# A spiking layer with a mixture of eight experts: two chains of term sums joined by a DMA, and the bias product read straight from PSUM one beat later

## The chip, the core and the metric

The kernel runs on one core of one Trainium2 chip. The metric is the device time of one execution in microseconds (us), lower is better. Engines are named as in the profile: PE is TensorE, PEld its weight loads, DVE is VectorE, ACT is ScalarE, POOL is GpSimd, SP is SyncE.

## The reference, cut to what matters

The input x has 16 sequences of 512 time steps with 256 channels. Per layer the reference computes:

```
R, K, V = x @ Wr.T, x @ Wk.T, x @ Wv.T
for t:  v += (in - v) * 0.5;  s = (v >= 1);  v *= 1 - s      # LIF, for r, k, v
        h = 0.9 * h + k * v;  y = r * h
x1  = layernorm(x + y @ Wo.T) * g1 + b1
s1  = lif_scan(x1 @ W1.T + b1)                               # 256 -> 1024
ffn = lif_scan(s1 @ W2.T + b2)                               # 1024 -> 256
x3  = layernorm(x + layernorm(x1 + ffn) * g2 + b2)
gates = softmax(x3 @ Wg + bg);  the two largest, normalised
out = sum over the two chosen experts e of gate_e * (x3 @ We[e] + be[e])
result = layernorm(x3 + out)
```

Everything is float32. The kernel multiplies all eight experts for every token and scales each by its gate, which is zero for six of them. The change lies in the last two lines: how the eight terms and the gated bias are added up to `res`, the input of the last layernorm.

## The kernel before, in words

**Chunks and beats.** Time is cut into 32 chunks of 16 steps; a chunk is 256 tokens (16 steps by 16 sequences), two tiles of 128. The whole kernel is a software pipeline of beats, k = -2 to 38. A chunk passes its stages in successive beats, and each stage has a lag: load of x (-2), R/K/V products (-1), LIF (0), attention output and LayerNorm 1 (1), W2 (3), LayerNorm 2 and 3 (LAG_Z, 5), experts (LAG_M, 6), final sum and last LayerNorm (LAG_F, 7). So in one beat TensorE works on the experts of chunk k-6 and VectorE on the final sum of chunk k-7. Beats 7 to 32 have all stages ("steady"); beats 33 to 38 lose one after the other ("drain"). Every engine has one hand-written order of work per beat (its `beat` function), and semaphores count stages.

**VectorE's slots.** VectorE runs the LIF recurrence, 32 instructions per beat (16 `membrane`, L723, and 16 `reset`, L730), and after each of them a slot of side work (`side`, slots -1 to 31). The tables STEADY, FILL and DRAIN say which side work stands in which slot. Of this: `y` in slots 0 to 4, `z_sum` and `fin_sum` in slot 5 (in the drain both in slot -1, with the spikes of h1, `s`, L1092, between them), `ln1_sum` (L831) in 7, `ln2_scale` in 16 and 17, the LN3 shift and `fin_add` in 24 (14 and 15 in the drain).

**The experts' terms.** Float32 products are made from split halves (hi and lo, float32r): three matmuls for each 128x128 block. Expert 0's product is scaled and added to x3 by VectorE into `acc` (`add_e0`, L937). ScalarE scales expert 1's product into `odd_sum` and the others' into `term` (`read_expert`, L596). GpSimd then adds them by DMA: terms 2, 4, 6 to `acc` (`add_even`, L1179) and terms 3, 5, 7 to `odd_sum` (`add_odd`, L1190), each an accumulating DMA of 256 KB from SBUF to SBUF that waits for the landing of the one before it in its chain. Terms 2 and 3 are added in the experts' beat, 4 to 7 in the beat after. The last chunk's terms are added by VectorE (`add_expert`, L950) in beat 37.

**The bias.** TensorE multiplies the transposed gates by the stacked expert biases (`biases`, L471) into `ps_zx`, behind expert 7, the last work of its beat. `ps_zx` is one PSUM bank with three users in turn: the transposes of z for LayerNorm 2 (`z_T`, tile `ps_zx<-cst,z`, L393), the transposes of x3 (`ps_zx<-cst,x`), and the bias.

**The final sum** (`fin_stage`). Step 0, `fin_sum` (L969): VectorE adds `ps_zx` to term 7 in SBUF; it waits for the bias and for all terms. TensorE's `z_T` of that beat waits for it, and so does the odd add of term 7. Step 1, `fin_add` (L976): `res = acc + odd_sum`, after both chains have landed. Steps 2 to 4: statistics, their aggregate (L810), the shift (L822); in between GpSimd computes the reciprocal deviation (L1147, L1149). ScalarE normalises `res` and sends it out. In the last beat, 38, the final sum is `res = acc + ps_zx` (L963).

**GpSimd's order in a steady beat**: spikes of h1 (L1161), add_even 4, add_odd 5, the DMA of the residual x into xb (L1195), reciprocal of LN1, add_even 6, reciprocal of LN2, add_odd 7, reciprocal of LN3, add_even 2, reciprocal of the final one, add_odd 3, the low half of the next x (L1168). In the drain the spikes are VectorE's.

## Time and profile before

| | us |
|---|---|
| median of 3 runs | 1047.85 |
| lowest, highest | 1046.26, 1048.25 |
| profiled execution, its own time | 1046.27 |
| span of its instructions | 1044.5 |
| mean granted TensorE clock | 0.969 of full speed |

A row of the timeline gives the start of a group of instructions in us from the span's start, its length, engine, line, operation and output<-input, and in brackets the idle time of the engine before it with what ended it. A row of the groups of lines has the count, the busy time in us, the mean of one in ns, and the idle time before them. Accumulating DMAs are issued by GpSimd (0.9 us of its time each) and land some time later; the landing is when their semaphore has its full count. Ends of matmuls are modelled, so rows of TensorE that follow each other overlap a little.

### The profile page before, as it was taken

Reading aid. Unit: us, or ns where it says so; the run is one execution under the profiler, and the core shown is the slowest. Engines: PE = TensorE matmul, PEld = TensorE weight load, DVE = VectorE, ACT = ScalarE, POOL = GpSimd, SP = SyncE. Lnnn points to the kernel's source line nnn. Section 1 sums busy time; section 2 is a strip of 40 time slices with the busy share of each in tenths; the row PEclk is TensorE's granted clock in tenths of the full one; section 3 lists DMA queues with packets and bytes.
Section 4 is the critical chain, followed back from the end, with each engine's and each line's share of the span. In section 5 each row is a group of like instructions: output and inputs, shape, how many; then the busy total and the mean of one; then the engine's idle time right before and its main releaser. Section 6 shows DMA issues by size and latency. Waiting matters only on the chain.

```text
span 1044.5 us, 22651 instructions
## 1 busy us (share of the span) xinstructions
PE 954.2 (91%) x7552; PEld 926.6 (89%) x7552; DVE 955.0 (91%) x3860; ACT 543.0 (52%) x1256; POOL 576.8 (55%) x720
## 2 busy tenths in 40 slices
PE   4577779999999999999999999999999999899884
PEld 4567769999999999999999999999999999889784
DVE  6888898999999999999999999999999999988875
ACT  4333333455666555555666555555566555456461
POOL 1001122676666666677666666667666666764551
PEclk8878888999999999999999999999999999999998
DMA  4310112454445445444445545444445554446762
GB/s 159 97 51 31 31 41 52 73 110 92 92 91 112 102 102 109 97 101 98 89 88 112 102 105 108 99 95 99 92 87 109 102 109 95 91 92 117 138 128 65
DMA packets 53110, 98.30 MB, mean 94 GB/s; under 512 B 5889, under 2 KB 5889, under 8 KB 52993
## 3 DMA queue, kind: packets, MB, share of 16 engines
q0 software_dynamic: 31392, 57.16, 31.6%
q1 hardware_dynamic: 16992, 31.30, 9.7%
q10 hardware_dynamic: 4608, 8.39, 2.1%
q8 instruction: 60, 0.98, 0.4%
q14 instruction: 58, 0.47, 0.1%
HBM read 31.29 MB, written 8.39 MB: 38 GB/s over the span
## 4 chain that ended last, share of the span: by engine, by line
PE 68%; DVE 17%; ACT 5%; DMA 5%; issue 3%; POOL 2%; POOLq 0%; DVEq 0%; SPq 0%; ACTq 0%
PE ps_e L349 25%; PE ps_proj L349 11%; PE ps_proj L419 9%; PE ps_proj L404 7%; PE ps_attn L385 6%; PE ps_proj L425 5%; DVE U L723 4%; DVE V L730 3%; DMA acc<-term 3%; ACT odd_sum L596 2%; PE ps_zx L393 2%; DVE stats L804 2%; DVE h L774 2%; ACT x_hi L577 1%; DVE x1n L831 1%
## 5 line engine op out<-in xcount | busy, mean ns | idle before, releaser
L349 PE MATMUL ps_e<-we_hi,x_hi 128*128 128x256 f32 (+1 forms) x1024 | 295.5, 289 | 16.8 <-ACT odd_sum L596 14.9
L349 PE MATMUL ps_e<-we_lo,x_hi 128*128 128x256 f32 (+1 forms) x1024 | 286.9, 280 | 0.0
L349 PE MATMUL ps_e<-we_hi,x_lo 128*128 128x256 f32 (+1 forms) x1024 | 286.7, 280 | 0.0
L730 DVE SCALAR_TENSOR_TENSOR V<-U 128x256 f32<-128x256 f32 (+5 forms) x656 | 243.3, 381 | 0.6
L723 DVE SCALAR_TENSOR_TENSOR U<-V,U 128x256 f32<-128x256 f32 (+5 forms) x656 | 234.0, 367 | 1.8
L559 ACT ACTIVATE U<-ps_proj,cst 128x256 f32<-128x256 f32 x320 | 135.6, 481 | 167.4 <-PE ps_proj L425 83.9
L1147 POOL TENSOR_SCALAR veps<-mv 128x2 f32<-128x2 f32 x128 | 55.7, 435 | 300.4 <-DVE mv L810 300.0
L349 PEld LDWEIGHTS ps_e<-we_hi,x_hi 128*128 128x128 f32 x1024 | 192.5, 188 | 23.0 <-ACT odd_sum L596 20.9
L1161 POOL TENSOR_SCALAR s<-U 128x256 fp32r<-128x256 f32 x208 | 192.0, 948 | 13.4 <-DVE V L730 13.4
L349 PEld LDWEIGHTS ps_e<-we_hi,x_lo 128*128 128x128 f32 x1024 | 192.9, 188 | 0.1
L349 PEld LDWEIGHTS ps_e<-we_lo,x_hi 128*128 128x128 f32 x1024 | 192.3, 188 | 0.0
L596 ACT ACTIVATE term<-ps_e,gate 128x256 f32<-128x256 f32 x372 | 157.0, 478 | 49.6 <-PE ps_e L349 49.3
L547 ACT ACTIVATE U<-ps_proj 128x512 f32<-128x512 f32 x96 | 57.5, 599 | 185.3 <-PE ps_proj L349 178.7
L419 PE MATMUL ps_proj<-x_hi,w_hi 128*128 128x256 f32 x512 | 135.3, 285 | 6.4 <-ACT x_hi L577 6.4
L419 PE MATMUL ps_proj<-x_hi,w_lo 128*128 128x256 f32 x512 | 134.2, 283 | 0.0
L404 PE MATMUL ps_proj<-s,w_hi 128*128 128x256 f32 x512 | 122.2, 280 | 2.9 <-POOL s L1161 2.9
L349 PE MATMUL ps_proj<-x_hi,wrkv_hi 128*128 128x256 f32 x384 | 114.2, 298 | 9.0 <-DVE wrkv_lo L1130 6.2
L404 PE MATMUL ps_proj<-s,w_lo 128*128 128x256 f32 x512 | 121.8, 279 | 0.0
L425 PE MATMUL ps_proj<-x_lo,w_hi 128*128 128x256 f32 x512 | 106.8, 290 | 4.0 <-DVE x_lo L852 3.9
L774 DVE SCALAR_TENSOR_TENSOR h<-h,kv 128x32 f32<-128x32 f32 x512 | 109.1, 213 | 1.4 <-DVE kv L767 0.5
L349 PE MATMUL ps_proj<-x_hi,wrkv_lo 128*128 128x256 f32 x384 | 110.0, 286 | 0.0
L349 PE MATMUL ps_proj<-x_lo,wrkv_hi 128*128 128x256 f32 x384 | 109.9, 286 | 0.0
(87 smaller groups left out, 2182.3 us busy)
## 6 DMA issues: line engine op xcount, KB each, us to landing
acc<-term POOLq DMA_DIRECT2D x93, 256.0 KB, 3.6
odd_sum<-term POOLq DMA_DIRECT2D x93, 256.0 KB, 3.3
xt<-x_T SPq DMA_DIRECT2D x33, 256.0 KB, 3.0
xa<-x_tok SPq DMA_DIRECT2D x32, 256.0 KB, 4.3
xb<-cst SPq DMA_DIRECT2D x32, 256.0 KB, 2.3
xb<-x_tok POOLq DMA_DIRECT2D x32, 256.0 KB, 6.2
out<-res ACTq DMA_DIRECT2D x32, 256.0 KB, 2.1
term<-w SPq DMA_DIRECT2D x8, 256.0 KB, 5.5
```

The source lines that it names most:

```text
L349: mm = pe.matmul(dst, lhs, rhs, start=(i == 0), stop=(i == n - 1))
L385: mm = pe.matmul(ps_attn[:, j, :], y[:, k * N + j * P:k * N + (j + 1) * P], wo[:, k, :], start=(k == 0), stop=(k == DK - 1))
L404: mm = pe.matmul(ps_proj[:, bank, e, :], wp[:, c:c + P], s1[:, ft, :], start=(ft == 0 and part == 0), stop=(ft == FK - 1 and part == 1))
L419: pe.matmul(ps_proj[:, bank, e, :], wp[:, cols(k, e)], x1_hi[:, k, :], start=(k == 0 and wp is w1_hi), stop=False)
L425: mm = pe.matmul(ps_proj[:, bank, e, :], w1_hi[:, cols(k, e)], x1_lo[:, k, :], start=False, stop=(k == DK - 1))
L547: return nc.scalar.activation(out_, in_, ACT.Identity)
L559: last = nc.scalar.activation(dst[:, :, col + e * B:col + (e + 1) * B], ps_proj[:, bank, e, :].rearrange("p (t b) -> p t b", b=B), ACT.Ide ...
L596: last = nc.scalar.activation(dst[:, j * D:(j + 1) * D], ps_e[:, bank, j, :], ACT.Identity, scale=gate[:, b.slot(LAG_M, 2), j, e:e + 1])
L723: v.scalar_tensor_tensor(out=U[:, s, t, c0:c1], in0=V[:, c0:c1], scalar=0.5, in1=U[:, s, t, c0:c1], op0=ALU.mult, op1=ALU.add).then_inc(do ...
L730: v.scalar_tensor_tensor(out=V[:, c0:c1], in0=u, scalar=THRESHOLD, in1=u, op0=ALU.is_lt, op1=ALU.mult).then_inc(done, 1)
L774: op = v.scalar_tensor_tensor(out=h[:, t, :], in0=h[:, (t - 1) % STEPS, :], scalar=DECAY, in1=kv[:, t, :], op0=ALU.mult, op1=ALU.add)
L1161: last = g.tensor_scalar(s1[:, ft, :].rearrange("p (t b) -> p t b", b=B), U[:, (b.k - 1) % 2, :, COL_H1 + ft * B:COL_H1 + (ft + 1) * B], T ...
```

## The change

- `fin_sum` is gone from VectorE and from the three slot tables; FIN_STEPS goes from 7 to 6.
- GpSimd has a new step `join`, right behind the odd add of term 7 and ahead of the reciprocal of LN3: it waits for the last landing of both chains and then adds `odd_sum` to `acc` by one more accumulating DMA of 256 KB. The odd add of term 7 no longer waits for `fin_sum`.
- The final sum is now `res = acc + ps_zx` in all beats; it waits for the bias and for the join's landing (in beat 38 for the terms).
- The bias product moves on TensorE from the end of the experts' beat to the next beat, between expert 3 and W1, and waits there until `ln2_scale` has read both tiles of `ps_zx`. The last chunk's stays in beat 37, ahead of expert 7, and waits for the final sum of the chunk before.
- `z_T` no longer waits for the sum of the chunk in LAG_F; the transposes of x3 now do, since the bias stands in `ps_zx` until the final sum has read it.

```diff
-STEADY = dict(y=(0, 1, 2, 3, 4), z_sum=5, spikes_h1=7, fin_sum=5,
+STEADY = dict(y=(0, 1, 2, 3, 4), z_sum=5, spikes_h1=7,
...
-FILL = dict(z_sum=-1, y=(-1,) * 5, spikes_h1=-1, fin_sum=-1,
+FILL = dict(z_sum=-1, y=(-1,) * 5, spikes_h1=-1,
...
-DRAIN = dict(z_sum=-1, y=(-1,) * 5, spikes_h1=-1, fin_sum=-1,
+DRAIN = dict(z_sum=-1, y=(-1,) * 5, spikes_h1=-1,
...
@@ -267,9 +267,10 @@
         gateT_done, gateT_ready, bias_done = sem("gateT_done"), sem("gateT_ready"), sem("bias_done")
         e0_added, term_ready = sem("e0_added"), sem("term_ready")
         even_added, odd_added = sem("even_added"), sem("odd_added")
+        joined = sem("joined")
         fin_steps, x3_ready, res_ready = sem("fin_steps"), sem("x3_ready"), sem("res_ready")
 
-        Y_STEPS, LN1_STEPS, LN2_STEPS, LN3_STEPS, GATE_STEPS, FIN_STEPS = 2, 7, 8, 5, 15, 7
+        Y_STEPS, LN1_STEPS, LN2_STEPS, LN3_STEPS, GATE_STEPS, FIN_STEPS = 2, 7, 8, 5, 15, 6
         ADDED = 16 * (E // 2 - 1)
         GATES_DONE = 13
 
@@ -459,13 +460,15 @@
                     mm = pe.transpose(ps_attn[0:STACK, j, 0:P], gate_parts[:, j, :].bitcast(F32), ident)
                 mm.then_inc(gateT_done, 1)
 
-            def biases(b):
-
-                pe.wait_ge(gateT_ready, b.value(1, LAG_M, 1))
+            def biases(b, lag):
+
+                pe.wait_ge(gateT_ready, b.value(1, lag, 1))
 
                 if b.has(LAG_Z):
-                    pe.wait_ge(x3_lo_ready, b.value(1, LAG_Z, 1))
-                if b.k == LAG_M:
+                    pe.wait_ge(ln2_steps, b.value(LN2_STEPS, LAG_Z, 6))
+                if lag == LAG_M:
+                    pe.wait_ge(fin_steps, b.value(FIN_STEPS, LAG_F, 1))
+                if b.k == LAG_F:
                     pe.wait_ge(bias_lo_ready, 1)
                 for j in range(TILES):
                     mm = pe.matmul(ps_zx[:, j, :], gate_T[:, j, :], bias_stack[:], start=True, stop=True)
@@ -474,8 +477,6 @@
             def z_T(b):
 
                 pe.wait_ge(z_ready, b.value(2, LAG_Z, 2))
-                if b.has(LAG_F):
-                    pe.wait_ge(fin_steps, b.value(FIN_STEPS, LAG_F, 1))
                 transpose4(ps_zx, lambda j, k: z[:, k, j * P:(j + 1) * P], zT_done)
 
             def beat(b):
@@ -519,6 +520,8 @@
                 if b.has(LAG_M):
                     for e in (2, 3):
                         expert(b, e)
+                if b.has(LAG_F) and b.k < LAST_BEAT:
+                    biases(b, LAG_F)
                 if b.has(LAG_Y):
                     if b.k == LAG_Y:
                         pe.wait_ge(split_lo, W1_PIECES)
@@ -528,15 +531,15 @@
                 if b.has(LAG_Z):
 
                     pe.wait_ge(x3_ready, b.value(1, LAG_Z, 1))
+                    if b.has(LAG_F):
+                        pe.wait_ge(fin_steps, b.value(FIN_STEPS, LAG_F, 1))
                     transpose4(ps_zx, lambda k, j: x3[:, j, k * P:(k + 1) * P], x3T_done)
                 if b.has(LAG_M):
                     gates_T(b)
                     for e in (5, 6, 7):
                         if e == 7 and b.last_m:
-                            biases(b)
+                            biases(b, LAG_M)
                         expert(b, e)
-                    if not b.last_m:
-                        biases(b)
 
             run_beats(beat)
 
@@ -954,33 +957,22 @@
 
             def fin_stage(b, step):
                 chain = lambda n: after(fin_steps, FIN_STEPS, LAG_F, b, n)
-                if step == 0 and b.k == LAST_BEAT:
-                    return
-                if step == 1 and b.k == LAST_BEAT:
+                if step == 1:
                     dve.wait_ge(bias_done, b.value(1, LAG_F, 1))
-                    dve.wait_ge(term_ready, b.value(E - 1, LAG_F, E - 1))
-                    dve.wait_ge(out_stored, b.value(16, LAG_F))
-                    v.tensor_tensor(res[:], acc[:, b.slot(LAG_F, 2)], ps_zx[:], ALU.add).then_inc(fin_steps, 2)
-                    return
-                if step == 0:
-                    dve.wait_ge(bias_done, b.value(1, LAG_F, 1))
-                    dve.wait_ge(term_ready, b.value(E - 1, LAG_F, E - 1))
-                    last_term = term[:, E - 3, 0:PIECE].rearrange("p (j d) -> p j d", j=TILES)
-                    v.tensor_tensor(last_term, last_term, ps_zx[:], ALU.add).then_inc(fin_steps, 1)
-                if step == 1:
-                    dve.wait_ge(even_added, b.value(ADDED, LAG_F, ADDED))
-                    dve.wait_ge(odd_added, b.value(ADDED, LAG_F, ADDED))
+                    if b.k == LAST_BEAT:
+                        dve.wait_ge(term_ready, b.value(E - 1, LAG_F, E - 1))
+                    else:
+                        dve.wait_ge(joined, b.value(16, LAG_F, 16))
 
                     if some(b.value(16, LAG_F)):
                         dve.wait_ge(out_stored, b.value(16, LAG_F))
-                    v.tensor_tensor(res[:], acc[:, b.slot(LAG_F, 2)], odd_sum[:, b.slot(LAG_F, 2)],
-                                    ALU.add).then_inc(fin_steps, 1)
+                    v.tensor_tensor(res[:], acc[:, b.slot(LAG_F, 2)], ps_zx[:], ALU.add).then_inc(fin_steps, 1)
                 if step == 2:
-                    chain(2)
+                    chain(1)
                     for j in range(TILES):
                         bn_stats(3, j, res[:, j, :], fin_steps)
                 if step == 3:
-                    bn_aggr(b, 3, fin_steps, FIN_STEPS, LAG_F, 4)
+                    bn_aggr(b, 3, fin_steps, FIN_STEPS, LAG_F, 3)
                 if step == 4:
                     mean_shift(b, 3, fin_steps, LAG_F)
 
@@ -1008,8 +1000,6 @@
                             y_stage(b, step)
                 if b.has(LAG_S) and b.dve_spikes and slot == at["spikes_h1"]:
                     spikes_h1(b)
-                if b.has(LAG_F) and slot == at["fin_sum"]:
-                    fin_stage(b, 0)
                 if b.has(LAG_Z):
                     for j in range(TILES):
                         if slot == at["ln2_stats"][j]:
@@ -1185,10 +1175,16 @@
 
                 if some(b.value(ADDED, lag, 16 * (e // 2 - 1))):
                     pool.wait_ge(odd_added, b.value(ADDED, lag, 16 * (e // 2 - 1)))
-                if e == E - 1:
-                    pool.wait_ge(fin_steps, b.value(FIN_STEPS, lag, 1))
                 g.dma_start(odd_sum[:, b.slot(lag, 2)].rearrange("p j d -> p (j d)"), term[:, e - 2, 0:PIECE],
                             accum_op=ALU.add).then_inc(odd_added, 16)
+
+            def join(b):
+
+                pool.wait_ge(even_added, b.value(ADDED, LAG_F, ADDED))
+                pool.wait_ge(odd_added, b.value(ADDED, LAG_F, ADDED))
+                g.dma_start(acc[:, b.slot(LAG_F, 2)].rearrange("p j d -> p (j d)"),
+                            odd_sum[:, b.slot(LAG_F, 2)].rearrange("p j d -> p (j d)"),
+                            accum_op=ALU.add).then_inc(joined, 16)
 
             def add_bias(b):
                 pool.wait_ge(xb_loaded, b.value(16, LAG_Z, 16))
@@ -1215,12 +1211,13 @@
                     reciprocal_std(b, 1, ln2_steps, LN2_STEPS, LAG_Z, 4)
                 if sums:
                     add_odd(b, LAG_F, 7)
+                    join(b)
                 if has_z:
                     reciprocal_std(b, 2, ln3_steps, LN3_STEPS, LAG_Z, 4)
                 if has_m and not b.last_m:
                     add_even(b, LAG_M, 2)
                 if has_f:
-                    reciprocal_std(b, 3, fin_steps, FIN_STEPS, LAG_F, 6)
+                    reciprocal_std(b, 3, fin_steps, FIN_STEPS, LAG_F, 5)
                 if has_m and not b.last_m:
                     add_odd(b, LAG_M, 3)
                 if b.has(LAG_X):
```

## Rows read from the trace of the kernel before

**Rows 1.** Page, part 1: busy us, share of the span and instructions of TensorE and VectorE.

```profile
PE 954.2 (91%) x7552; PEld 926.6 (89%) x7552; DVE 955.0 (91%) x3860; ACT 543.0 (52%) x1256; POOL 576.8 (55%) x720
```

**Rows 2.** Windows, 328 to 884 us; columns as the first line names them.

```profile
core 0: us, PE busy (x) PEld busy (x) DVE busy (x) ACT busy (x) POOL busy (x), PEclk, DMA share, GB/s
328.00:884.00 556.00, 547.87 (x4478) 537.72 (x4477) 533.78 (x2068) 315.59 (x740) 369.55 (x456) 1.00 0.48 100
```

**Rows 3.** Waits, 328 to 884 us: us in total, times, longest us.

```profile
DVE x1n L831 <- PE ps_attn L385: 9.8, 17, 0.6
...
PE ps_e L349 <- ACT odd_sum L596: 8.1, 19, 0.4
```

**Rows 4.** Timeline, VectorE's final sums of beats 33 to 37: start us, us.

```profile
959.55 0.68 DVE L976 TENSOR_TENSOR res<-acc,odd_sum 128x512 f32<-128x512 f32 x1
...
978.16 0.69 DVE L976 TENSOR_TENSOR res<-acc,odd_sum 128x512 f32<-128x512 f32 x1
...
995.63 0.69 DVE L976 TENSOR_TENSOR res<-acc,odd_sum 128x512 f32<-128x512 f32 x1
...
1011.66 0.69 DVE L976 TENSOR_TENSOR res<-acc,odd_sum 128x512 f32<-128x512 f32 x1
...
1026.94 0.68 DVE L976 TENSOR_TENSOR res<-acc,odd_sum 128x512 f32<-128x512 f32 x1
```

**Rows 5.** Timeline, TensorE, its wait in beat 34 (idle us before, releaser).

```profile
970.24 0.63 PE L393 MATMUL ps_zx<-cst,z 128*128 128x128 f32 x4 [2.90 <-DVE term L969]
```

**Rows 6.** Groups of lines, VectorE: xcount | busy us, mean ns.

```profile
L969 DVE TENSOR_TENSOR term<-term,ps_zx 128x512 f32<-128x512 f32 x31 | 20.9, 676 | 8.2 <-ACT term L596 8.2
...
L963 DVE TENSOR_TENSOR res<-acc,ps_zx 128x512 f32<-128x512 f32 x1 | 0.7, 689 | 1.7 <-DMA out<-res 1.7
```

**Rows 7.** Timeline, VectorE, one steady beat: final sum, then y.

```profile
503.89 0.69 DVE L976 TENSOR_TENSOR res<-acc,odd_sum 128x512 f32<-128x512 f32 x1
...
513.35 0.94 DVE L797 SCALAR_TENSOR_TENSOR y<-U,h 128x256 f32<-128x256 f32 x2
```

**Rows 8.** Timeline, TensorE, the same beat: transposes of x3, then projection.

```profile
506.49 0.60 PE L393 MATMUL ps_zx<-cst,x 128*128 128x128 f32 x4
...
515.90 1.89 PE L385 MATMUL ps_attn<-wo,y 128*128 128x256 f32 x8
```

**Rows 9.** Timeline, GpSimd: issues of term 7's odd add.

```profile
495.74 0.93 POOL L1190 DMA_DIRECT2D odd_sum<-term  x1
...
953.23 0.92 POOL L1190 DMA_DIRECT2D odd_sum<-term  x1
...
973.50 0.93 POOL L1190 DMA_DIRECT2D odd_sum<-term  x1
```

**Rows 10.** Line L1190, issue to landing: 200 to 900 us, then beats 33 to 37.

```profile
DMA to landing us min/median/max: 3.2/3.3/6.4
...
DMA to landing us min/median/max: 5.5/5.5/5.5
...
DMA to landing us min/median/max: 3.5/3.5/3.5
...
DMA to landing us min/median/max: 3.9/3.9/3.9
...
DMA to landing us min/median/max: 4.2/4.2/4.2
...
DMA to landing us min/median/max: 3.2/3.2/3.2
```

**Rows 11.** Chain of waits, beat 35 into 36: start us, us, what.

```profile
998.49 3.30 DMA odd_sum<-term
...
1001.83 0.49 issue
```

**Rows 12.** Timeline, VectorE, beat 34: spikes of h1, then the LN2 statistics.

```profile
967.59 1.91 DVE L1092 TENSOR_SCALAR s<-U 128x256 fp32r<-128x256 f32 x8
...
970.91 0.43 DVE L804 BATCH_NORM_STATS2 stats<-ps_zx 128x6 f32<-128x256 f32 x1 [0.63 <-PE ps_zx L393]
```

## The prediction, made before the changed kernel ran

> **What bounds the kernel now.** I read the page's busy shares first. TensorE and VectorE are both busy 91% of the span [rows 1], so the shares alone do not say which one sets the time. The table of windows, asked for the even middle of the run (328 to 884 us, 19 beats), says more: TensorE is busy 547.87 of 556 us at full granted clock, VectorE 533.78 [rows 2]. The list of waits for the same window names TensorE's pauses: 8.1 us over 19 times, all for ScalarE's read of expert 1 (L596), which is 0.43 us in each beat. VectorE, in turn, waits 9.8 us for TensorE's output projection [rows 3]. So in a steady beat (some 29.3 us, 556 / 19) TensorE works back to back, VectorE follows it and has about a microsecond to spare. ScalarE's read of expert 1 comes behind TensorE's transposes of x1n; VectorE's fin_sum (L969) is nowhere in that chain.
>
> The last beats are different. The starts of the final sum (L976) in beats 33 to 37 are 18.6, 17.5, 16.0 and 15.3 us apart [rows 4]: with stages dropping out, no engine is full, and the beat is a chain through VectorE, GpSimd's queue and its accumulating DMAs. In beat 34 TensorE even stands 2.90 us still for fin_sum before it can transpose z [rows 5]. That is where a change of waits can be seen.
>
> **The change, part by part.**
>
> *Removed from VectorE: fin_sum, the add of the bias product into term 7.* 31 times 0.676 us, 20.9 us of busy time [rows 6]. In the steady beats this lies beside TensorE's work. VectorE reaches its next wait on TensorE (L831) 0.6 us sooner and waits 0.6 us longer; behind that wait nothing has moved. I cost it at zero there. If TensorE did not cover it, it would give up to 0.43 us a beat, no more, since TensorE has no more idle time.
>
> *The final sum reads ps_zx in place of odd_sum.* The kernel has both kinds of read already: with two SBUF tiles L976 takes 0.68 or 0.69 us [rows 4], and the one in the last beat with PSUM (L963) takes 0.689 us [rows 6]. Cost: zero.
>
> *The bias product one beat later.* The same two matmuls per chunk, now behind expert 3 and ahead of W1. They wait for ln2_scale to have read ps_zx, and VectorE has done this well before in a steady beat. TensorE's work is the same: zero. The new wait of the x3 transposes for the final sum has these in its way: they start at 506.49 in the beat whose final sum starts at 503.89 and takes 0.69 [rows 7, 8], so the sum may be 1.9 us late before TensorE feels it. The other limit is y: it is written by 514.29 (513.35 + 0.94) and TensorE wants it at 515.90 [rows 7, 8], 1.6 us of slack.
>
> *The join: one more accumulating DMA of 256 KB per chunk on GpSimd's queue.* It waits for the last odd add to land, costs the queue an issue (0.93 us, as the add's own [rows 9]), and the final sum waits for its landing. Three prices. (a) The flight of an odd add, issue to landing: 3.2 / 3.3 / 6.4 us (least, median, most) in the middle of the run [rows 10]. Nothing else of GpSimd's is in flight with the join, so I take 3.3 from the median; the ends are 3.2 and 6.4. (b) From a landing to the issue behind it: in the chain of waits, 3.30 us of flight from 998.49, then 0.49 us of "issue" from 1001.83, then the next add [rows 11]; I take 0.5. (c) 0.1 from the landing to VectorE.
>
> *A steady beat.* The odd add of term 7 is issued at 495.74 [rows 9]. It lands at 499.0, the join is issued at 499.5 and lands at 502.8, 1.1 us before the final sum at 503.89. Hidden. GpSimd is free again by 500.5; the reciprocals it holds up (ln3's, then the final one) are asked for later than that. A join late by up to 1.6 us is absorbed as well. So beats 7 to 32: zero.
>
> The Trainium skill (DMA: Bandwidth & Descriptors, Anatomy of one DMA) fits a GpSimd-issued DMA by 2.0 us plus bytes over 436e3 per us. For 256 KB that is an estimate of 2.6 us, while the trace shows 3.3. With 2.6 the join would be 0.7 us cheaper in each of the last beats.
>
> *The last beats.* The odd add of term 7 lands here just before the final sum, and the join has no room. Neither has the work behind it: GpSimd's ln3 reciprocal now waits behind the join too, but is back earlier than the join has landed.
> - Beat 33: issued 953.23 [rows 9], flight 5.5 [rows 10], 0.5, join 3.3, 0.1: the final sum starts at 962.6, against 959.55 [rows 4]. Late by 3.1 us. VectorE is dense from there to the spikes of beat 34, which end at 972.6 in place of 969.50 (967.59 + 1.91) [rows 12]. Here the change gives something back: fin_sum (0.6) is gone and TensorE transposes z while the spikes run, so the LN2 statistics start behind the spikes and the logits, at 972.9 in place of 970.91 [rows 12]: 2.0 late.
> - Beat 34: issued at 973.50 + 2.0, flight 3.5 [rows 9, 10], then 0.5 + 3.3 + 0.1: the final sum at 982.9 against 978.16, 4.7 late.
> - Beats 35 to 37: now a loop through the queue decides. Final sum to the odd add of term 3 takes 2.9 us (995.63 to 998.49, through GpSimd's reciprocal), then term 5 after 3.3 + 0.5, then term 7 after 3.3 + 0.5, its flight f, 0.5, the join 3.3, 0.1: together 14.4 + f, in place of intervals of 17.5, 16.0 and 15.3 [rows 4, 11]. With f = 3.9, 4.2 and 3.2 [rows 10] the final sums fall at 982.9 + 18.3 = 1001.2, + 18.6 = 1019.8 and + 17.6 = 1037.4. Against 995.63, 1011.66 and 1026.94 that is 5.6, 8.1 and 10.5 late. In beat 37 VectorE's own add of experts 4 to 7 stands behind the final sum in its queue, and so do TensorE's experts 6 and 7 and the last output: the delay goes to the end in full.
>
> **Sum:** 0 in beats -2 to 32, +10.5 us in beats 33 to 37. The profiled execution took 1046.27 us (span 1044.5), which makes 1056.8; the median of the three runs is 1.58 above it, so 1058.4.
>
> **Rivals.**
> 1. *The join is late in the steady beats too.* Place: VectorE's slot 24 in 26 beats. If it flew 5.5 us and more, as adds do that share the engines, the final sum would start 1.1 us late and more; from 1.6 us on, y is late and each beat pays. At the 6.4 of [rows 10] that is 499.5 + 6.4 + 0.1 - 503.89 = 2.1, so 0.5 us a beat, 13 us, and the last beats pay 3.1 more for each of five joins, 15.5: 1087. A middle course (5.5, nothing steady, 5 x 2.2 in the end) gives 1069. For it: the DMA engines carry one more transfer. Against: adds with a free queue fly 3.3.
> 2. *Faster: the drain gains.* If the last beats' waits overlap more than I think and the join falls under other waiting, the gain is TensorE's wait for fin_sum in beat 34, 2.90 us [rows 5]: 1045. It decides if the last odd add lands over 3.9 us before VectorE comes to the final sum. The rows speak against this: in beat 34 it lands at 977.0, 1.2 us before.
> 3. *VectorE, not TensorE, sets the steady beat.* Then fin_sum's 0.6 us comes back up to TensorE's idle 0.43: 26 x 0.43 = 11, less the loss in the end: about no change, 1047. Against: TensorE's pause waits for ScalarE alone [rows 3].
> 4. *Only one join is paid.* If the queue's loop does not close and the lag stays at beat 34's 4.7: 1052.5.
>
> **How the numbers follow.** The forecast has 0.62, the long flights (1) 0.12, the small loss (4) 0.12, no change (3) 0.07, the gain (2) 0.07. This kernel's measurement can tell about 0.2% (2.1 us) from nothing. Slower by more: 0.62 + 0.12 + 0.12 = 0.86. The forecast's own range is 1055 to 1063: flights of 4.2 in place of 3.3 add 4.5 in five joins, and a give-back of 2.90 in one more beat takes 3 off. To hold 8 in 10 I reach down to rival 4 and up to the middle course of rival 1: 1051 to 1068.
>
> **What would show it.** Right: in the steady beats the final sum starts without idle time before it and the beat stays 29.3; TensorE's waits there are ScalarE's 0.43 alone. From beat 33 on the final sum shows idle time that ends with the DMA acc<-odd_sum, some 1 to 5 us each, and the starts of the final sum in beats 34 to 37 are about 18 us apart. GpSimd shows a wait of 2.4 us for the odd add's landing before each join, and TensorE none for fin_sum. Wrong: steady beats of another length, an idle GpSimd queue behind the join that holds up ln3's shift on VectorE in steady beats, or last beats of the old length.

## The result, and the profile after

The changed kernel takes 1093.88 us (median of 4 runs, 1092.66 to 1094.57) against 1048.05 us: ratio 1.0427, 95% interval [1.0405, 1.0449]. The forecast was 1058.4, with 1068 as its upper end: slower, as forecast, but by 45.8 us in place of 10.5. The profiled execution took 1094.57 us, its span is 1092.7.

Where the 48.2 us of span came from is read from the starts of the final sums (L969 after, L976 before), which cut both spans at the same work:

| stretch | before | after | difference |
|---|---|---|---|
| start to final sum of beat 7 | 211.0 | 213.5 | +2.5 |
| to that of beat 30 (23 steady beats) | 673.6 | 710.9 | +37.2 |
| to that of beat 32 | 54.7 | 56.7 | +2.1 |
| to that of beat 37 | 87.6 | 97.2 | +9.5 |
| to the end of the span | 17.6 | 14.4 | -3.2 |

A steady beat now takes 30.91 us on the mean (710.9 / 23); it took 29.29. The windows of the changed kernel, 328 to 884 us, as in [rows 2]:

```profile
328.00:884.00 556.00, 526.17 (x4246) 513.90 (x4245) 516.63 (x1943) 298.91 (x702) 370.49 (x450) 0.99 0.51 103
```

TensorE was busy 547.87 of these 556 us and is now busy 526.17; VectorE went down too, and the granted clock is 0.99 where it was 1.00. Nobody is full, so the beat is set by a chain of waits. The waits of the same window (engine, line, what it waited for: us in total, times, longest):

```profile
POOL acc L1185 <- DMA odd_sum<-term: 54.0, 17, 4.0
...
POOL s L1151 <- DVE V L733: 29.5, 18, 2.1
...
PEld ps_e L350 <- DVE x_lo L864: 23.7, 13, 2.0
DVE res L969 <- issue: 22.2, 14, 2.5
PE ps_e L350 <- DVE x_lo L864: 21.0, 13, 1.8
...
DVE x1n L834 <- PE ps_attn L386: 5.3, 6, 1.2
...
PE ps_e L350 <- ACT odd_sum L599: 7.9, 18, 0.6
```

The last two answer to [rows 3]: ScalarE's 0.43 us a beat is still there, VectorE's wait for the projection has halved. New are TensorE's 21.0 us for the low half of x3 (behind the final sum on VectorE), VectorE's 22.2 us ahead of the final sum ("issue" means that the profile names no releaser; in 19 of the 23 steady beats the sum starts 0.08 us after the join's landing), and 29.5 us of GpSimd's spikes for VectorE's last reset. The join's flight, line L1185, from 200 to 910 us and then in one drain beat:

```profile
DMA to landing us min/median/max: 3.3/4.7/5.5
...
DMA to landing us min/median/max: 3.3/3.3/3.3
```

**The closed loop.** The chain of waits from one final sum to the next (start us, us, what) shows what none of the prediction's steps had:

```profile
400.52 0.69 DVE res L969
...
403.36 0.74 POOL rstd L1139
...
404.20 0.93 POOL odd_sum L1178
405.14 1.34 POOL x_lo L1158
406.47 2.07 issue
...
408.58 1.18 POOL s L1151 x2
...
415.99 4.45 DMA acc<-term
...
420.98 0.93 POOL acc L1169
...
422.99 3.29 DMA odd_sum<-term
...
426.81 3.34 DMA acc<-odd_sum
...
431.56 0.69 DVE res L969
```

The final sum stands in VectorE's slot 24; the resets behind it end the beat's recurrence; GpSimd's spikes wait for the last reset; adds 4, 6 and 7 stand behind the spikes on GpSimd's queue; the join behind them; the next final sum behind the join. So nothing in this chain is fixed by TensorE, and a late join moves its own next start. Its terms, against the same in the kernel before (final sums at 474.59 and 503.89):

| from | to | before | after |
|---|---|---|---|
| final sum | spikes start | 6.67 | 8.06 |
| | even add 4 issued | 7.34 | 7.41 |
| | odd add 7 issued | 7.14 | 7.00 |
| | its landing, + 0.5, join issued | (3.8) | 3.82 |
| | join lands, final sum starts | (3.4) | 4.75 |
| sum | | (28.35) | 31.04 |

In brackets the prices of the prediction. With those the loop would take 28.35 us, under the beat of 29.3. Two terms grew, 1.4 us each. By this sum either of them alone would be enough to put it over (29.7).

*The join flies 4.7 us and not 3.3.* SyncE starts two loads beside it. Its queue beside the join of the loop above:

```profile
426.80 0.47 SPq L337 DMA_DIRECT2D xb<-cst  x1
427.31 0.59 SPq L310 DMA_DIRECT2D xt<-x_T  x1
```

What they cost hangs on the order of the two. In the steady beats of the changed kernel, e2 and e5 (experiments below) 34 joins are issued 0.45 us or more ahead of SyncE's first load and fly 3.3 us at the median (3.26 to 4.45); 39 are issued later than that, and they fly 4.7 (3.63 to 5.49). In the old trace the first load starts at 500.56. The join that the prediction put at 499.5 is 1.1 us ahead of it, on the good side; a join that comes 0.7 us or more later is not.

*VectorE is held by GpSimd.* The timeline of VectorE, then of GpSimd, in the same beat:

```profile
404.35 2.41 DVE L733 SCALAR_TENSOR_TENSOR V<-U 128x256 f32<-128x256 f32 x1
406.80 0.42 DVE L726 SCALAR_TENSOR_TENSOR U<-V,U 128x256 f32<-128x256 f32 x1
...
407.47 0.68 DVE L864 TENSOR_TENSOR x_lo<-ps_zx,x_hi 128x512 fp32r<-128x512 f32 x1
```

```profile
404.84 1.64 POOL L1158 TENSOR_TENSOR x_lo<-xt,x_hi 128x512 fp32r<-128x512 f32 x1
...
408.58 7.46 POOL L1151 TENSOR_SCALAR s<-U 128x256 fp32r<-128x256 f32 x8 [2.11 <-DVE V L733]
```

A reset takes 0.42 us; this one takes 2.41 and ends with GpSimd's split of the next x (404.84 + 1.64 = 406.48, then 0.3). The kernel before has the same split, but it begins just as VectorE's own x_lo does, which reads PSUM and one SBUF tile and is not lengthened; the reset behind it stretches to 1.00. (In 4 of its 23 steady beats the split meets `kv`, L764, instead, which takes 1.3 us and not 0.23.)

```profile
508.86 0.69 DVE L861 TENSOR_TENSOR x_lo<-ps_zx,x_hi 128x512 fp32r<-128x512 f32 x1
509.46 1.00 DVE L730 SCALAR_TENSOR_TENSOR V<-U 128x256 f32<-128x256 f32 x1
```

```profile
508.89 1.29 POOL L1168 TENSOR_TENSOR x_lo<-xt,x_hi 128x512 fp32r<-128x512 f32 x1 [0.38 <-ACT x_hi L547]
```

Why it meets a reset now is seen from the times since the final sum's start, 400.52 after and 503.89 before. ScalarE's x_hi of the next x, which the split needs, is ready at 3.5 us and not at 4.9: the sum has fallen back against TensorE's and ScalarE's work (the transposes of x3 start 1.2 us behind it and not 2.6).

```profile
403.40 0.64 ACT L550 ACTIVATE x_hi<-xt 128x512 fp32r<-128x512 f32 x1
```

```profile
508.16 0.64 ACT L547 ACTIVATE x_hi<-xt 128x512 fp32r<-128x512 f32 x1
```

So GpSimd no longer waits for it and starts the split at 4.3 us, right behind the add of term 3, where it started at 5.0. VectorE's x_lo has its place at 5.0 us in both kernels; the split now begins ahead of it and holds the reset before it, and x_lo comes at 6.95. Of 21 steady beats, 15 have such a step of over 1.5 us; before, no step of the recurrence has. The Trainium skill (GPSIMD Engine Reference, section Specifications) says that GpSimd's SBUF interfaces are shared with VectorE and that instructions of VectorE with two SBUF inputs, or in a two-port mode, contend. The trace agrees: the reset takes both inputs from SBUF and is held, the subtract with a PSUM input beside the same split takes 0.69. Whether `kv`, which has one input, runs in such a mode is not shown here.

**A ring that feeds itself.** Both grown terms come of a final sum that is late: it delays the next join into SyncE's loads, and it lets the split begin ahead of x_lo. Each makes the next final sum late. With neither, the loop is under TensorE's beat (29.20 in e7, which takes both away); once late, it tends to stay late. Which of the two came first in the fill of the pipeline is not shown: the first steady beat already has both, a step of 1.96 us and a flight of 4.90.

### The profile page after: what moved, and what is told of

Same layout as the page of the kernel before. It is cut to its first block, busy times and chain, and to the rows that moved or that the text cites. A ratio compares the mean times of both kernels' runs of the same rounds, so it can differ in the third digit from the quotient of the medians.

```text
span 1092.7 us, 22650 instructions
## 1 busy us (share of the span) xinstructions
PE 968.0 (89%) x7552; PEld 936.7 (86%) x7552; DVE 965.4 (88%) x3829; ACT 541.8 (50%) x1256; POOL 610.4 (56%) x751
## 4 chain that ended last, share of the span: by engine, by line
POOL 23%; DVE 22%; DMA 21%; PE 19%; issue 12%; ACT 2%; POOLq 0%; DVEq 0%; SPq 0%; ACTq 0%
POOL s L1151 12%; DMA odd_sum<-term 8%; DMA acc<-odd_sum 7%; DMA acc<-term 6%; PE ps_e L350 6%; DVE V L733 5%; DVE U L726 4%; PE ps_proj L350 4%; POOL rstd L1139 3%; PE ps_attn L386 3%; PE ps_proj L405 3%; DVE stats L807 3%; POOL x_lo L1158 2%; DVE h L777 2%; POOL acc L1169 2%
## 5 line engine op out<-in xcount | busy, mean ns | idle before, releaser
L350 PE MATMUL ps_e<-we_hi,x_hi 128*128 128x256 f32 (+1 forms) x1024 | 300.1, 293 | 44.0 <-DVE x_lo L864 26.4
L350 PE MATMUL ps_e<-we_hi,x_lo 128*128 128x256 f32 (+1 forms) x1024 | 289.8, 283 | 0.0
L733 DVE SCALAR_TENSOR_TENSOR V<-U 128x256 f32<-128x256 f32 (+5 forms) x656 | 260.6, 407 | 0.6
L726 DVE SCALAR_TENSOR_TENSOR U<-V,U 128x256 f32<-128x256 f32 (+5 forms) x656 | 240.9, 377 | 1.8
L350 PEld LDWEIGHTS ps_e<-we_hi,x_hi 128*128 128x128 f32 x1024 | 195.4, 191 | 53.9 <-DVE x_lo L864 29.9
L350 PEld LDWEIGHTS ps_e<-we_hi,x_lo 128*128 128x128 f32 x1024 | 195.5, 191 | 0.1
L350 PEld LDWEIGHTS ps_e<-we_lo,x_hi 128*128 128x128 f32 x1024 | 195.3, 191 | 0.0
L1137 POOL TENSOR_SCALAR veps<-mv 128x2 f32<-128x2 f32 x128 | 58.6, 457 | 202.0 <-DVE mv L813 201.9
L1139 POOL TENSOR_TENSOR rstd<-veps,neg_half 128x2 f32<-128x2 f32 x128 | 104.8, 819 | 10.7
```

The lines of the kernel that those rows point to most:

```text
L350: mm = pe.matmul(dst, lhs, rhs, start=(i == 0), stop=(i == n - 1))
L726: v.scalar_tensor_tensor(out=U[:, s, t, c0:c1], in0=V[:, c0:c1], scalar=0.5, in1=U[:, s, t, c0:c1], op0=ALU.mult, op1=ALU.add).then_inc(do ...
L733: v.scalar_tensor_tensor(out=V[:, c0:c1], in0=u, scalar=THRESHOLD, in1=u, op0=ALU.is_lt, op1=ALU.mult).then_inc(done, 1)
L1137: g.tensor_scalar(veps[ln][:], mv[ln][:, :, 1], EPS, None, ALU.add).then_inc(rstd_ready[ln], 1)
L1139: g.tensor_tensor(rstd[ln][:], veps[ln][:], neg_half[:], ALU.pow).then_inc(rstd_ready[ln], 1)
```

## The experiments

Each compares with the kernel before on its own chip. "Steady beat" is the mean of the 23 from final sum 7 to final sum 30, "last beats" the time from that of beat 32 to that of beat 37.

| kernel | ratio, 95% interval | steady beat | last beats | longest step of VectorE's recurrence in a beat (median of 21) |
|---|---|---|---|---|
| before | | 29.29 | 87.6 | 1.01 |
| after | 1.0427 [1.0405, 1.0449] | 30.91 | 97.2 | 2.41 |
| e1_no_join | 0.9951 [0.9925, 0.9976] | 29.18 | 86.6 | 1.08 |
| e2_ungated | 1.0004 [0.998, 1.0028] | 29.19 | 94.9 | 1.09 |
| e3_loads_late | 1.0096 [1.006, 1.0133] | 29.38 | 98.9 | 1.02 |
| e5_thin_split | 0.9991 [0.9969, 1.0013] | 29.19 | 97.7 | 0.64 |
| e7_loads_thin | 0.999 [0.9969, 1.0011] | 29.20 | 100.0 | 0.63 |
| e8_quarter_join | 1.0064 [1.0038, 1.009] | 29.50 | 94.0 | 1.02 |
| e6_thin_before | 0.993 [0.9909, 0.9951] | 29.28 | 88.7 | 0.64 |
| e4_two_adds | 1.0167 [1.0144, 1.0189] | 29.88 | 88.2 | 1.96 |
| e10_two_adds_thin | 0.9929 [0.9898, 0.9961] | 29.18 | 91.4 | 0.63 |
| e9_pair | 1.0044 [1.0026, 1.0061] | 29.20 | 91.9 | 1.13 |
| e11_mixed | 1.0028 [1.0004, 1.0053] | 29.22 | 89.7 | 1.10 |
| e12_more_issues | 0.9996 [0.9978, 1.0015] | 29.27 | 87.7 | 1.00 |

**e1_no_join: the change without its join.** The odd terms are left out of the result.

```diff
-                        dve.wait_ge(joined, b.value(16, LAG_F, 16))
+                        dve.wait_ge(even_added, b.value(ADDED, LAG_F, ADDED))
+                        dve.wait_ge(odd_added, b.value(ADDED, LAG_F, ADDED))
...
-                    join(b)
```

> The changed kernel without the join DMA: the final sum waits for the last landing of both chains, as before, and adds acc and ps_zx; the odd terms are left out of the result. Theory (closed loop): the cost comes from the final sum waiting for one more DMA in a loop that runs final sum, VectorE's last reset, GpSimd's spikes, the adds of terms 4, 6 and 7, final sum. Without the join the loop has 4 us of slack again: steady beats of 29.3 us and a total of 1043 to 1048. Rival (the moved bias product and TensorE's new waits cost the time): beats stay at 31.0 and the total near 1090.

1043.6 us. All the rest of the change together gives some 4 us; the join costs 50. Most of the profiled gain of 3.0 is in the steady beats (23 x 0.11 = 2.5), where TensorE's pause is unchanged but its W1 block takes 5.66 us and not 5.76. Its first two matmuls on x1's low half take 0.40 us there and 0.50 before, so the bias product probably fills what was a short wait for that half; no run tests it.

**e2_ungated: the join is there, but nobody's sum waits for it.** It goes into a spare tile, and the odd terms are left out.

```diff
-                g.dma_start(acc[:, b.slot(LAG_F, 2)].rearrange("p j d -> p (j d)"),
+                g.dma_start(spare[:], odd_sum[:, b.slot(LAG_F, 2)].rearrange("p j d -> p (j d)"),
```

> The changed kernel with the join kept in its place in GpSimd's queue, with its wait, its issue and its 256 KB, but it adds odd_sum to a spare tile and the final sum does not wait for it (it waits for both chains' landings and adds acc and ps_zx; the odd terms are left out). Theory (closed loop through the final sum): 1044 to 1050, beats of 29.3. Rival (the join holds up GpSimd's queue or loads the DMA engines): near 1090, beats of 31.

1049.24 us. In the steady beats the transfer and the queue cost nothing (29.19): the final sum's wait does it all. The join itself flies 4.3 us there (median), and it does no harm. In the last beats it is the other way round: they take 94.9 us, so 8.3 of the 10.6 us that the changed kernel has over e1 are there without any gate. There GpSimd stands at the join until the odd add has landed, and LayerNorm 3's reciprocal is queued behind it; VectorE needs that reciprocal for the shift that stands ahead of its final sum. Waits from 939 to 1034 us:

```profile
POOL spare L1192 <- issue: 18.8, 5, 5.5
...
DVE shift L829 <- POOL rstd L1144: 9.4, 8, 2.5
```

The second was 2.3 us in the last beats of e1, and in those of the changed kernel itself (981 to 1078 us) it is nearly as long as here:

```profile
DVE shift L825 <- POOL rstd L1140: 2.3, 5, 1.2
```

```profile
DVE shift L825 <- POOL rstd L1139: 8.3, 8, 2.6
```

**e3_loads_late: SyncE's two loads wait until the join has landed.**

```diff
+                    if b.has(LAG_F) and b.k < LAST_BEAT:
+                        sp.wait_ge(joined, b.value(16, LAG_F, 16))
```

> The changed kernel, but SP issues its two loads of the beat (xb from the constants, the next x) only after the join has landed. In the changed kernel they are issued within 0.5 us of the join, and its flight is 4.7 us in most steady beats. Theory: with the engines to itself the join flies 3.3 us, the loop shortens by 1.4 us to 29.6 or less, 24 beats give back some 34 us: 1055 to 1063. Rival (the flight is long for another reason, or the flight is not what sets the beat): over 1085.

1059.15 us: the join flies 3.3 us again (median of the page) and 35 of the 46 us are back. The held step is gone as well, though the split is whole: 2 of the 23 steady beats have one of over 1.5 us, where the changed kernel has 17. The last beats stay long.

**e5_thin_split: the changed kernel with GpSimd's split cut to 8 of 256 columns** after the first chunk; the low parts of x are left out of the R/K/V product.

```diff
-                g.tensor_tensor(x_lo[:], xt[:, b.slot(LAG_X, 2)], x_hi[:].bitcast(F32),
+                c = slice(None) if b.k == LAG_X else slice(0, 8)
+                g.tensor_tensor(x_lo[:, :, c], xt[:, b.slot(LAG_X, 2), :, c], x_hi[:, :, c].bitcast(F32),
```

> The changed kernel with GpSimd's split of the next x (tile x_lo<-xt,x_hi) cut from 256 to 8 columns per row block (the other low parts are left out of the result after the first chunk). In the changed kernel one VectorE reset or membrane step of a beat lasts 1.96 to 2.41 us in place of 0.42, and ends with GpSimd's split. Theory (GpSimd's two-input work holds VectorE, and this closes the loop): that long step is gone, the final sum comes 2 us sooner behind the spikes, steady beats fall from 31.0 to 29.2; with the last beats' loss of some 7 us: 1048 to 1056. Rival (the long step is only where VectorE waits for something else, the join's flight alone makes the beat): 1085 or more.

1046.76 us, below what either theory gave, and 29.19 a steady beat with all bytes of the join in it. The long flight is gone as well, though SyncE's loads are as they were: 3.3 us at the median. In beats 20 to 25, behind one whose join was issued 1.3 us late, it flies 4.6 to 4.9, and these beats still take 29.2 on the mean: with no step held, the spikes start 6.1 us behind the sum and not 8.1. Line L733 from 328 to 884 us (duration ns least/median/most), after and then here:

```profile
L733 DVE SCALAR_TENSOR_TENSOR V<-U x288: 380/415/2419, 329.0 to 883.9; 128x256 f32<-128x256 f32 x144
```

```profile
L733 DVE SCALAR_TENSOR_TENSOR V<-U x305: 384/415/452, 328.9 to 883.4; 128x256 f32<-128x256 f32 x153
```

**e7_loads_thin: both cuts.** The low parts of x are left out as in e5.

> The changed kernel with both cuts: SP's loads held until the join has landed, and GpSimd's x_lo split thin (the low parts of x left out). With the thin split alone the beats were at 29.2 and the time 1046.8, so TensorE sets the beat already and the second cut finds nothing left in the steady beats: 1045 to 1048. If SP's loads beside the join cost in the drain too, up to 1 us a beat there goes: 1042 to 1045. If the late loads cost by themselves (the few beats of over 30 us in the run with late loads alone), 1048 to 1054.

1047.3 us, as the first case has it. So either cut is enough, and both together find no more than the thin split alone. That does not give a price to each: e3 and e5 each took the other grown term away too, as a ring does when it is opened at one place. Late loads make the last beats no shorter; the join flew 3.3 there already.

**e6_thin_before: the same thin split in the kernel before.** The low parts of x are left out.

> The kernel before with GpSimd's x_lo split cut to 8 of 256 columns after the first chunk; the low parts of x are then left out of the product. If the long hold of VectorE matters only where the final sum is tied to the odd add, nothing changes here: TensorE sets the beat at 29.3 us, VectorE gains idle time of about 0.7 us a beat that nobody uses, and the time stays at 1045 to 1049. If the split's work is a cost by itself in any kernel of this shape, and the run of the changed kernel with a thin split was fast for that reason alone, this one gains as well: 1000 to 1030 us.

1040.24 us: outside both ranges. The steady beats are as they were (29.28); of the 3.6 us of span gained, 3.75 lie before the final sum of beat 7 (207.25 and not 211.00), where the pipeline fills. A thin split is therefore worth 0.7% by itself, and the price of the changed kernel's design with it is 1046.76 - 1040.24 = 6.5 us, against 45.8 without. The other 39 us went with the hold and what it fed; what is left is in the last beats (97.7 and not 88.7, less 3.1 at the very end).

**e8_quarter_join: the join moves 128 of 512 columns.** The rest of the odd terms is left out.

```diff
-                g.dma_start(acc[:, b.slot(LAG_F, 2)].rearrange("p j d -> p (j d)"),
-                            odd_sum[:, b.slot(LAG_F, 2)].rearrange("p j d -> p (j d)"),
+                g.dma_start(acc[:, b.slot(LAG_F, 2), 0, 0:D // 2], odd_sum[:, b.slot(LAG_F, 2), 0, 0:D // 2],
```

> The changed kernel with the join cut to a quarter of its bytes (128 of 512 columns; the other odd terms are left out), all waits kept. Theory (closed loop): the join's flight falls from 4.7 to 2.5 us or less, the loop from 31.0 to under 29.2, so steady beats as before and half of the last beats' loss: 1044 to 1054. Rival (what costs is one more issue and wait in GpSimd's queue): over 1075.

1053.93 us. The flight falls only to 2.4 us at the least and 3.6 at the median, and the beats waver between 28.7 and 30.8. 7 of 21 beats still have the long step. Cutting the bytes does not cut the wait in proportion.

**e4_two_adds: no join; the bias product late, then two adds on VectorE in slot 24.** All terms are in.

```diff
+                    if not last:
+                        chain(1)
+                        v.tensor_tensor(res[:], res[:], odd_sum[:, b.slot(LAG_F, 2)], ALU.add).then_inc(fin_steps, 1)
...
-                    join(b)
```

> The bias part of the change alone: no join, the bias product one beat later, the final sum on VectorE as two adds in a row at the old place (acc + ps_zx, then + odd_sum). All terms are in the result. Theory (the join alone costs): 1044 to 1049; the second add costs VectorE 0.7 us in a slot with about 1 us to spare, and TensorE no longer waits for fin_sum in the last beats, some 2 us. Rival (moving the bias costs): over 1080.

1066.45 us, a miss. No DMA stands before the final sum here, and yet 22 of the 23 steady beats take 29.9 us, each with one membrane step held for 1.96 us:

```profile
516.93 1.96 DVE L726 SCALAR_TENSOR_TENSOR U<-V,U 128x256 f32<-128x256 f32 x1
```

```profile
516.97 1.63 POOL L1163 TENSOR_TENSOR x_lo<-xt,x_hi 128x512 fp32r<-128x512 f32 x1
```

That is the hold without the join, so it does not need the join's loop: VectorE has one more add per beat here, and the split begins ahead of x_lo again.

**e10_two_adds_thin: the same with the thin split.** The low parts of x are left out.

> The kernel of two adds (no join) with the same thin split on GpSimd. With the full split it took 1066 against my forecast of 1044 to 1049, in beats of 29.9 us in which VectorE idles 0.69 us and one membrane step lasts 1.96 us. Theory (VectorE is full: the second add's 0.6 us, and a longer hold by the split): without the hold VectorE has 1 us to spare, beats of 29.2, total 1042 to 1048. Rival (the second add costs by itself, its wait or its place): 1055 or more.

1040.92 us, ratio 0.9929, steady beats 29.18: e4's whole loss in the steady beats was the hold. It stands level with e6 (1040.24 and 1040.92), so it is no gain over the order of before either.

**e9_pair: the join early.** VectorE adds term 6 to term 7 in SBUF in slot 5, GpSimd adds the pair to `acc` in the place of term 6, and `odd_sum`, complete after term 5, is joined at once. All terms are in, and the queue has as many DMAs as before.

```diff
+                if step == 0:
+                    v.tensor_tensor(term[:, E - 3, 0:PIECE], term[:, E - 3, 0:PIECE], term[:, E - 4, 0:PIECE],
+                                    ALU.add).then_inc(fin_steps, 1)
...
-                    add_even(b, LAG_F, 6)
+                    add_pair(b)
```

> A version meant to beat both, all terms in: the bias product late and read by the final sum as in the change, but VectorE adds term 6 to term 7 at the old place of fin_sum (slot 5), GpSimd adds the pair to acc in the place of term 6's add and then joins odd_sum (terms 1, 3, 5) to acc. As many DMAs and VectorE adds as the kernel before, and the last landing is some 3 us ahead of the final sum. Theory: steady beats of 29.2 as in the run without the join, last beats about as before: 1042 to 1048, faster than the kernel before by 0 to 0.5%. Rival (any join in front of the final sum is late): over 1060.

1051.61 us. The steady beats are right (29.20): one flight fewer stands between the spikes and the final sum, and the join lands ahead of it in each (2.1 us at the median). The last beats are not (91.9).

**e11_mixed: e9 up to beat 32, e4's two adds from beat 33 on.** All terms are in.

> All terms are in. Up to beat 32 this is the pair form (term 6 added to term 7 on VectorE early in the beat, the pair sent into acc, then an early join): that form ran its steady beats at 29.2 us and its last beats slowly. In beats 33 to 37 there is no join at all: the final sum adds acc and the bias product, then odd_sum, as before the change. If the drain's cost is the join's flight standing before each final sum, it goes: final sum of beat 32 at 937 to 939 and 105 to 106.5 us from there to the end, against 109.2 in the pair form and 111.6 in the changed kernel, so 1043.5 to 1047 us. If the extra VectorE sum or something else of the drain (the bias product read late) costs it instead, 109 us remain and the time stays at 1050 to 1053.

1050.93 us, and 89.7 us for the last beats: 2.2 less than e9, 2.1 more than before. No version with all terms in beats the kernel before. What the remaining 2 us are was not tracked down.

**e12_more_issues: the kernel before with 31 tiny DMAs more.** This one asks about the end of the program; see the last section.

```diff
+                if -1 <= b.k <= 2:
+                    for i in range(8 * (b.k + 1), min(8 * (b.k + 2), 31)):
+                        g.dma_start(spare[:, 2 * i:2 * i + 2], neg_half[:]).then_inc(filled, 16)
```

> The kernel before with 31 tiny extra DMAs (128 rows of 8 bytes each, into a spare tile) issued by GpSimd in beats -1 to 2, where it has nothing else to do: 249 DMAs on its queue, as many as the changed kernel has, in place of 218. GpSimd's DRAIN at the end of the program took 7.25 us in every kernel with 218 of them and 3.29 us in every one with 249, and ScalarE is done 3 us before the longer one ends. If the number of DMAs decides, the DRAIN takes 3.29 us here, the last final sum is followed by 6.7 us instead of 9.6, and the time falls by 3 us to 1043.5 to 1046. If it is what the late joins leave behind at the end, the DRAIN stays at 7.25 us and the time at 1046 to 1050. The issues, 29 us of GpSimd's time in its idle beginning, cost at most 1 to 3 us if they hold up the first reciprocals.

1045.83 us, ratio 0.9996: no change.

## Why the prediction was wrong, step by step

- **What bounds the kernel before**: right. e1 and e6 give or take VectorE time and the steady beat stays at TensorE's 29.2 to 29.3.
- **fin_sum removed, zero; the sum's PSUM read, zero**: right. L969 takes 0.69 us, as in [rows 4, 6], and e1 shows no more than TensorE's own gain.
- **The bias moved, zero**: nearly right, some 2.5 us better than that (e1).
- **"A steady beat", the step that failed**: "Hidden. [...] So beats 7 to 32: zero". It measured +37.2 in 23 beats. It went wrong in two ways.
  - The frame. It took the issue of term 7's add at 495.74 as given and asked how late the join may be against the final sum, with slack of 1.1 and 1.6 us. But the issue itself hangs on the final sum before it, by way of the last reset and the spikes. There is no slack against one's own past: what counts is whether the whole round, 28.35 us by the prediction's own prices, is shorter than 29.3. The true slack was 0.95 us a round.
  - The sizes. They were right for a join that is on time, and were taken as fixed. "Nothing of GpSimd's is in flight with the join, so I take 3.3" looked at one queue only: a join that is late meets SyncE's loads, and flies 4.7. And a late sum lets GpSimd's split hold a step of VectorE, 2.41 us in place of 0.42, for which the sum had no term at all. The hold was in the old trace as a reset of 1.00 us. So the round grew to 31.04.
- **The last beats**: near in size (9.5 us against 10.5), but by another wait in the main. The forecast had intervals of 20.3, 18.3, 18.6 and 17.6 us from beat 33 on; the timeline of the changed kernel has 20.3, 19.5, 19.5 and 17.7:

```profile
1001.34 0.69 DVE L969 TENSOR_TENSOR res<-acc,ps_zx 128x512 f32<-128x512 f32 x1 [0.84 <-issue]
...
1021.68 0.69 DVE L969 TENSOR_TENSOR res<-acc,ps_zx 128x512 f32<-128x512 f32 x1 [1.10 <-PE ps_zx L474]
...
1041.17 0.69 DVE L969 TENSOR_TENSOR res<-acc,ps_zx 128x512 f32<-128x512 f32 x1 [1.19 <-issue]
...
1060.67 0.69 DVE L969 TENSOR_TENSOR res<-acc,ps_zx 128x512 f32<-128x512 f32 x1 [1.24 <-DMA acc<-odd_sum]
...
1078.32 0.69 DVE L969 TENSOR_TENSOR res<-acc,ps_zx 128x512 f32<-128x512 f32 x1 [1.61 <-issue]
```

  The join's 3.3 us there was exact. The idle time ahead of these sums, in brackets, is 0.8 to 1.6 us, where the forecast had 1 to 5. For the forecast has the final sum wait for that flight, and says that LayerNorm 3's reciprocal is back in time. It is not: e2, where no sum waits for the join, has 8.3 of the 10.6 us, and VectorE's wait for that reciprocal went from 2.3 us (e1) to 8.3. Most of the cost is GpSimd's wait ahead of the join and not the flight behind it; that the sizes agree is in part luck.
- **"The delay goes to the end in full"**: wrong by 3.2 us, which came back behind the last final sum (last section).
- **Rival 1** named the right place, "VectorE's slot 24 in 26 beats", and its list of signs was met: steady beats of another length. Its price (0.5 us a beat; measured 1.6) was again the excess over the slack, at a flight longer than the true one. The Trainium skill's fit (DMA: Bandwidth & Descriptors, Anatomy of one DMA) gives an estimate of 2.6 us for 256 KB; no whole join was so fast here, the least being 3.2.

## What to carry to other kernels

Before a wait is costed against slack in one beat of a pipeline, follow it once round: if the work it delays is an ancestor of the next round's same wait, add up the whole loop and compare that with the beat. Then ask what each term becomes when the loop runs late, since a term that grows with lateness can keep it late. Price a transfer's flight with what every queue has in flight at the moment when it will run, and a little later, not with the median of its kind. And where an elementwise step moves by a microsecond, look at what GpSimd runs beside it: a step that shares SBUF with GpSimd's can lengthen several times over, and whether it does hangs on the order of the two.

## What was not expected of the hardware

- **GpSimd's two-input op holds a VectorE step.** 0.42 us becomes 2.41 (reset) or 1.96 (membrane) beside a 128x512 subtract of GpSimd, whose own time goes from 1.29 to 1.64. Beside VectorE's op with one PSUM input neither is lengthened. In each steady beat of the kernels with the whole split some step of VectorE is lengthened; the order decides whether by half a microsecond or by 2.
- **A joined DMA costs more than its bytes.** 256 KB from SBUF to SBUF fly 3.3 us alone, or with the first of SyncE's two loads 0.45 us or more behind the issue, and 4.7 where that load comes earlier; a quarter of it takes 2.4 at the least and 3.6 at the median.
- **GpSimd's DRAIN at the end has two lengths.** Line L173, the program's end, before and then after:

```profile
L173 POOLq DRAIN  x1: 7250/7250/7250, 1037.0 to 1037.0; - x1
...
L173 ACTq COMPARE_BRANCH  x1: 33/33/33, 1041.2 to 1041.2; - x1
```

```profile
L173 POOLq DRAIN  x1: 3291/3291/3291, 1088.1 to 1088.1; - x1
...
L173 ACTq COMPARE_BRANCH  x1: 33/33/33, 1092.3 to 1092.3; - x1
```

  Before, it ends at 1044.3, 3 us after ScalarE is through with the last output; after, it ends first. That is the 3.2 us of the table. All runs read fall into these two: 7.25 in before, e1, e4, e6, e9, e10 and e11, with 218 DMAs issued by GpSimd, and 3.29 in after, e2, e3, e5, e7 and e8, with 249. The number is not the cause: e12 issues 249 in the kernel of before, and its DRAIN stays long.

```profile
L173 POOLq DRAIN  x1: 7245/7245/7245, 1038.4 to 1038.4; - x1
```

  What decides stays open.
